# Two PSUM banks for the small steps, two instead of three for the score units, and new places for the steps

## Time and profile before

| what | value |
|---|---|
| median of 3 runs | 1191.55 us (1189.46 to 1191.91) |
| the profiled execution | 1190.55 us |
| its span, first to last instruction | 1188.7 us |
| granted TensorE clock, mean over the span | 0.919 of 2.4 GHz |
| setup, pass -1 | 0 to 99 us |
| pass 0, layer 0 experts, passes 1 to 9 | 99 to 150, 150 to 217, 217 to 805 us |
| layer 1 experts, passes 10 to 15, end | 805 to 938, 938 to 1173, 1173 to 1189 us |

### The profile page before, as it was taken

One profiled execution on the slowest core, in us unless ns is written; L12 is line 12 of the kernel. 1 busy time (PEld: TensorE's weight loads), 2 busy tenths in 40 slices (PEclk: granted clock), 3 DMA queues, 4 the chain that ended last, 5 costly groups with the idle time before them and its releaser, 6 DMA issues.

```text
span 1188.7 us, 23248 instructions
## 1 busy us (share of the span) xinstructions
PE 1017.7 (86%) x7354; PEld 517.9 (44%) x7354; DVE 786.2 (66%) x2427; ACT 653.2 (55%) x1251; POOL 573.5 (48%) x651
## 2 busy tenths in 40 slices
PE   4879889988989898986788788875999989889986
PEld 2522279532333333331333234444889644444433
DVE  5588922578878787878666676683444577678931
ACT  1204722567757666655566565553344567667764
POOL 5184600246547373627858688742000155437663
PEclk8657989999989999988999899987999999999987
DMA  5852557652323041412214224233888545344411
GB/s 144 221 141 66 146 162 207 210 121 46 98 45 97 23 97 28 106 30 57 71 46 121 53 66 106 62 97 128 237 246 256 134 116 134 77 105 111 91 44 46
DMA packets 122540, 130.55 MB, mean 110 GB/s; under 512 B 13952, under 2 KB 105408, under 8 KB 122208
## 3 DMA queue, kind: packets, MB, share of 16 engines
q1 hardware_dynamic: 115856, 116.09, 37.6%
q0 software_dynamic: 6144, 12.60, 4.0%
q10 hardware_dynamic: 432, 0.52, 0.2%
HBM read 83.13 MB, written 52.48 MB: 114 GB/s over the span
## 4 chain that ended last, share of the span: by engine, by line
PE 46%; POOL 25%; DVE 9%; issue 7%; ACT 5%; DMA 5%; SPq 1%; POOLq 0%; ACTq 0%; DVEq 0%
PE ps_banks L610 6%; POOL tokens L995 5%; PE ps_banks L1719 5%; PE ps_banks L569 5%; PE ps_banks L576 4%; POOL sent L1915 3%; PE ps_banks L615 3%; PE ps_banks L693 3%; PE ps_banks L688 3%; DVE a_neg_max L834 3%; PE ps_banks L1460 2%; PE ps_banks L1474 2%; PE ps_banks L1732 2%; PE ps_banks L654 2%; DMA tokens<-made,at 2%
## 5 line engine op out<-in xcount | busy, mean ns | idle before, releaser
L834 DVE TENSOR_REDUCE a_neg_max<-ps_banks 128x1 f32<-128x512 f32 x512 | 325.6, 683 | 94.8 <-PE ps_banks L576 92.6
L737 ACT ACTIVATE a_probs<-ps_banks 128x512 f32<-128x512 f32 x512 | 283.9, 598 | 153.4 <-PE ps_banks L569 150.9
L576 PE MATMUL ps_banks<-k_strip,q_strip 51*128 51x512 bf16 (+3 forms) x1024 | 308.0, 364 | 30.2 <-DVE a_neg_max L834 27.0
L569 PE MATMUL ps_banks<-q_strip,k_strip 53*128 53x512 bf16 (+3 forms) x1024 | 291.1, 353 | 41.3 <-ACT a_probs L739 16.3
L840 DVE CUSTOM_DVE_ANT_0 a_masked<-ps_banks,mask_wide 128x384 bf16<-128x384 f32 (+3 forms) x512 | 221.7, 486 | 61.2 <-PE ps_banks L576 60.6
L739 ACT ACTIVATE a_probs<-ps_banks 128x512 f32<-128x512 f32 x256 | 144.9, 599 | 76.9 <-PE ps_banks L534 74.8
L576 PEld LDWEIGHTS ps_banks<-k_strip,q_strip 51*128 51x128 bf16 x1024 | 77.0, 95 | 185.7 <-ACT a_probs L737 115.3
L957 POOL CAST a_q_parts<-a_q_whole 128x512 bf16<-128x512 f32 x16 | 9.7, 608 | 296.9 <-ACT a_q_whole L770 296.9
L569 PEld LDWEIGHTS ps_banks<-q_strip,k_strip 53*128 53x128 bf16 x1024 | 75.6, 94 | 165.3 <-ACT a_probs L737 52.5
L610 PE MATMUL ps_banks<-a_probs,v_aug 128*32 128x512 f32 x1024 | 141.6, 626 | 0.0
L995 POOL DMA_INDIRECT tokens<-made,at x96 | 93.1, 969 | 27.9 <-issue 27.2
(11 more groups left out here) (248 smaller groups left out, 1680.9 us busy)
## 6 DMA issues: line engine op xcount, KB each, us to landing
work<-in_pack SPq DMA_DIRECT2D x40, 450.0 KB, 3.5
q_rows<-a_q_parts SPq DMA_DIRECT2D x96, 128.0 KB
k_rows<-a_k_parts SPq DMA_DIRECT2D x96, 128.0 KB
q_strip<-q_rows SPq DMA_DIRECT2D x64, 192.0 KB
k_strip<-k_rows SPq DMA_DIRECT2D x64, 192.0 KB
work<-in_w SPq DMA_DIRECT2D x32, 256.0 KB, 3.1
sent<-in_zeros SPq DMA_DIRECT2D x14, 512.0 KB, 7.6
work<-sent SPq DMA_DIRECT2D x56, 128.0 KB, 3.2
```

The lines of the kernel that those rows point to most:

```text
L569: mm = pe.matmul(sbank[:, at:at + hi - lo], k_now[rows(js, ROW_END), slot, kt * P:(kt + 1) * P], q_now[rows(js, ROW_END), slot, lo:hi], st ...
L576: mm = pe.matmul(mbank[:, at:at + hi - lo], q_next[rows(jm, ROW_SHIFT), slot, qt * P:(qt + 1) * P], k_next[rows(jm, ROW_SHIFT), slot, lo:h ...
L737: act.activation(probs[si // 4 % 2][:, si % 4, :], bank, ACT.Exp).then_inc(sems["probs"], 1)
L834: dve.tensor_reduce(neg_max[:, half, qt, hd:hd + 1], bank, AX.X, ALU.max, negate=True).then_inc(sems["max_out"], 1)
```

## The change

- **Banks.** Score units have 2 banks (0, 1), maximum units 3 (2 to 4), the small steps 2 (5, 6) and the sums bank 7. Small steps alternate between banks 5 and 6, each with its own semaphore (`misc_free0`, `misc_free1`); `claim` waits for the last reader of its own bank only. Where a step reads what the step before it had copied out, `after` waits for that copy. Where all must be read out, `all_free` waits for both.
- **Places.** In `MISC[0]`, `shift` is moved ahead of `norm`, `gather` from place 7 to 12 (after `ln1`, which goes from 9 to 10), `yT` from 15 to 16, `ff1` from 16, 17, 19, 20 to 17, 18, 20, 21, `ff2a`/`ff2` from 22, 23 to 23, 24, `ln2` from 25 to 27. In layer 1, `tanh`, `gz`, `mix` and `store` of passes 10 to 13 go from 23, 25, 26, 29 to 27, 28, 29, 31. The parts of the routing are moved by zero to three places.
- **Moments.** They are steps of their own, `pmom` (places 8 and 9) and `fmom` (places 25 and 26), half of the instructions in each; before, they followed the addition at once.
- **Matmuls of `q`, `k` and `ff1`** are issued as two of 256 columns in place of one of 512.
- **The end.** `final` is replaced by `tail_take`, `tail_norm`, `tail_turn`, `tail_out`, each in two halves with banks of its own, and the last `tanh` moves from place 28 to 31, after the last unit.

```diff
-BANKS, RING, MAX_BANK, SUM_BANK, MISC_BANK = 8, 3, 3, 6, 7
+BANKS, LAG, SCORE_RING, MAX_RING, MAX_BANK, MISC_BANK, SUM_BANK = 8, 3, 2, 3, 2, 5, 7
 MISC = {
-    0: {0: [("zTa", 2)], 1: [("ln3a", -2), ("zT", 2)], 2: [("norm", -1, QT - 1)], 3: [("ln3b", -2), ("shift", 0, 1)], 4: [("q", 2)],
-        5: [("onT", -1)], 6: [("k", 2)], 7: [("proj", -1), ("gather", -1)], 8: [("v", 1), ("load", 3)], 9: [("ln1", -1), ("x2T", -2)],
-        10: [("norm", 0, 0)], 11: [("logits", -2)], 12: [("z", 1)], 15: [("yT", -1)], 16: [("fetch", 2, 0), ("ff1", -1, 0)],
-        17: [("ff1", -1, 1)], 18: [("norm", 0, 1)], 19: [("ff1", -1, 2)], 20: [("ff1", -1, 3)], 21: [("shift", 1, 0)],
-        22: [("gate", -1), ("ff2a", -1)], 23: [("ff2", -1)], 24: [("tanh", -1)], 25: [("ln2", -1)], 26: [("norm", 0, 2), ("gz", -1)], 28: [("mix", -1)],
-        30: [("store", -1)]},
-    1: {0: [("zT", 2)], 2: [("shift", 0, 1)], 3: [("q", 2)], 4: [("norm", -1, QT - 1)], 5: [("k", 2)], 7: [("onT", -1)],
-        8: [("v", 1)], 10: [("proj", -1)], 12: [("norm", 0, 0)], 16: [("fetch", 2, 0)], 19: [("shift", 1, 0)], 20: [("norm", 0, 1)],
-        28: [("norm", 0, 2)]},
+    0: {0: [("zTa", 2)], 1: [("ln3a", -2), ("zT", 2)], 2: [("shift", 0, 1)], 3: [("ln3b", -2), ("norm", -1, QT - 1)], 4: [("q", 2)],
+        5: [("onT", -1)], 6: [("k", 2)], 7: [("proj", -1)], 8: [("pmom", -1, 0), ("v", 1), ("load", 3)], 9: [("pmom", -1, 1), ("x2T", -2)],
+        10: [("ln1", -1), ("z", 1)], 11: [("logits", -2)], 12: [("gather", -1), ("norm", 0, 0)], 16: [("yT", -1), ("fetch", 2, 0)],
+        17: [("ff1", -1, 0)], 18: [("ff1", -1, 1)], 19: [("norm", 0, 1)], 20: [("ff1", -1, 2)], 21: [("ff1", -1, 3)],
+        22: [("shift", 1, 0)], 23: [("gate", -1), ("ff2a", -1)], 24: [("ff2", -1)], 25: [("tanh", -1), ("fmom", -1, 0)], 26: [("fmom", -1, 1)],
+        27: [("ln2", -1), ("norm", 0, 2), ("gz", -1)], 29: [("mix", -1)], 31: [("store", -1)]},
+    1: {0: [("zT", 2)], 2: [("shift", 0, 1)], 3: [("norm", -1, QT - 1)], 4: [("q", 2)], 5: [("k", 2)], 7: [("onT", -1)],
+        8: [("v", 1)], 10: [("proj", -1)], 13: [("norm", 0, 0)], 16: [("fetch", 2, 0)], 19: [("shift", 1, 0)], 21: [("norm", 0, 1)],
+        29: [("norm", 0, 2)]},
 }
...
-    NB - 3: routed(0, (13, 14, 16, 19), 27, 29, 30, 28, 31),
-    NB - 2: sends(0, *4 * (0,), *4 * (16,), *4 * (30,)),
-    NB - 1: merged(routed(1, (12, 13, 15, 16), 18, 20, 21, 22, 24), sends(12, *4 * (16,), *4 * (30,))),
-    NB: sends(20, *4 * (17,)),
-    ROUTE1: merged(routed(2, (8, 9, 10, 11), 13, 15, 16, 18, 20), sends(24, *8 * (17,))),
-    **{MIX1 + i: mixed(-2, 8, 20, 23, 25, 26, 29) for i in range(4)},
-    MIX1 + 4: merged(mixed(-2, 0, 8, 11, 13, 14, 17), mixed(-1, 15, 24, 27, 29, 30, 31)),
-    STREAM - 1: merged(mixed(-1, 0, 8, 11, 13, 14, 17), mixed(0, 18, 25, 28, 30)),
+    NB - 3: routed(0, (13, 15, 18, 21), 25, 29, 30, 28, 31),
+    NB - 2: sends(0, *4 * (0,), *4 * (13,), *4 * (30,)),
+    NB - 1: merged(routed(1, (12, 13, 15, 16), 18, 21, 22, 23, 25), sends(12, *4 * (17,), *4 * (30,))),
+    NB: sends(20, *4 * (18,)),
+    ROUTE1: merged(routed(2, (8, 9, 10, 11), 14, 17, 18, 20, 22), sends(24, *8 * (19,))),
+    **{MIX1 + i: mixed(-2, 8, 20, 27, 28, 29, 31) for i in range(4)},
+    MIX1 + 4: merged(mixed(-2, 0, 8, 12, 13, 14, 17), mixed(-1, 15, 24, 30, 31, 31, 31)),
+    STREAM - 1: merged(mixed(-1, 0, 8, 14, 15, 16, 18), mixed(0, 19, 25, 31, 31)),
...
+        def all_free(eng, n):
+            for side in range(2):
+                wait(eng, misc_free[side], n.freed(side))
+        def after(eng, n, made):
+            if made in n.last:
+                side, count = n.last[made]
+                wait(eng, misc_free[side], count)
...
                 def claim():
-                    wait(pe, sems["misc_free"], n.at("misc_free"))
+                    wait(pe, misc_free[n.side()], n.freed(n.side()))
...
-                                wait(pe, sems["probs"], n.at("probs") - (RING - 1))
+                                wait(pe, sems["probs"], n.at("probs") - (SCORE_RING - 1))
...
                         if name in ("q", "k"):
+                            after(pe, n, "zT")
...
-                            pe.matmul(ps_misc, w_of[layer][name][:], z_T[par][:], start=True, stop=True).then_inc(sems["misc"], 1)
+                            for half in (slice(0, S // 2), slice(S // 2, S)):
+                                mm = pe.matmul(ps_misc[:, half], w_of[layer][name][:], z_T[par][:, half], start=True, stop=True)
+                            mm.then_inc(sems["misc"], 1)
...
-                            wait(dve, sems["misc_free"], n.at("misc_free") + 1)
-                            moments_of("ff2", t0, D, QT)
+                        if name == "fmom":
+                            if arg == 0:
+                                all_free(dve, n)
+                            op = moments_of("fmom", t0, D, 2 * arg, 2 * (arg + 1))
+                            if arg == 1:
+                                op.then_inc(sems["moments"], 1)
```

224 lines of the change are left out of this document (147 added, 77 removed).

## The result

The changed kernel takes 1184.37 us (median of 7 runs, 1183.05 to 1187.40); the kernel before took 1191.55 us (median of 7, 1189.46 to 1195.22). The ratio is 0.994, with a 95% interval from 0.9919 to 0.9962. So it is faster, but by 7 us (0.6%) and not by 25.

What follows compares the result with a forecast made beforehand. The prediction took PE to pace the kernel, counting where it stands still. Its terms, +8 - 9 - 9 - 10 - 6 + 1 = -25 us against 1190.55, gave 1165.5 us (1166 for a median), range 1150 to 1185.

Steps and rivals of the forecast that it cites:

- The end: Passes 14, 15 and tail: POOL's last gate stays, sums finish before it, copies and projection run in halves; -6 us.
- Rival 4: Groups without steps: short waits of the two-bank score ring drop PE to the low clock; +42 us, 1208; chance 0.12.
- Passes 10 to 13: Later `tanh` removes most of PE's stall and slow clock: -3.3 us in each of 10 to 12, 0 in 13; -10.
- +1.0 for the score ring: Passes 10 to 12: cost of two score banks in place of three, 1.0 us in each pass.
- Passes 1 to 4: Bank waits, `yT` wait, burst and slow clock go, the score ring costs 2.6 us: -2.2 us each, -9 in all.
- Groups 25, 26 and 27, 28 cost nothing, as DVE is later there: Passes 1 to 4, places 25 to 28: two score banks add no time, since DVE is later; 0 us.
- Pass 0: Few small steps, so two score banks cost 10.1 us, less two waits of `norm` at 1 us each; +8 us.
- Passes 5 to 9: Gathers moved behind `ln1` shorten the chain of PE, DVE and POOL: -8, -3.6, +1.2 and +1.5 us; -9 in all.
- +1.5: From pass 8 to the last `send`: late moments, `ln3a` blocking DVE in pass 9 and later `count`; +1.5 us.
- Rival 2: POOL takes the gains back: passes 5 to 9 give 0, passes 10 to 12 keep their stall; 1182 us; chance 0.15.
- Rival 1: Two score banks are as good as free, as DVE's maxima already hold every group; 1144 us; chance 0.12.
- Rival 3: The second bank for small steps brings nothing, since steps follow one another through their data; 1189 us; chance 0.04.

Runs made afterwards that it cites:

- d_fill: The changed kernel with one unneeded 512-column matmul after each score unit of pass 15, to keep PE busy: 1178.88 us, ratio 0.9925.
- c_wholemom: The changed kernel with both halves of the moments at the first of their two places: 1178.30 us, ratio 0.9926.
- a_oldbanks: The changed kernel with the banks of before, three for score units and one for small steps: 1180.99 us, ratio 0.9923.
- r_ring2: The changed kernel with two score banks but only one bank for small steps, bank 5 left empty: 1203.36 us, ratio 1.0106.
- after_again: The changed kernel once more, unchanged, for a second profile: 1183.06 us, ratio 0.9920.
- p_late9: The kernel with banks by pass, with pass 9's last moments and routing about four places later: 1296.53 us, ratio 1.0008, in the later runs.
- after_third: The changed kernel once more, unchanged, in the later runs: 1327.95 us, ratio 1.0241.
- x_mix: The changed kernel with the banks of before up to pass 4 and from pass 10, the new ones in passes 5 to 9: 1166.36 us, ratio 0.9796.

## Why the prediction was wrong

The direction was right, and the measured time lies inside the range, at its upper end; the size was three and a half times too large by the medians, four times by the profiles. By these, 25 forecast stand against 6.2 measured:

| step | forecast | measured |
|---|---|---|
| setup, pass -1 | 0 | +1.6 |
| pass 0 and the experts of layer 0 | +8 | +5.8 - 5.2 = +0.6 |
| passes 1 to 4 | -9 | -3.9 |
| passes 5 to 9 | -9 | -5.3 |
| experts of layer 1 | 0 | +1.6 |
| passes 10 to 13 | -10 | -4.5 |
| passes 14, 15, end | -6 | +3.7 |
| split | +1 | not to be told from 0 |

- **The end (9.7 us off) is the step that failed most**, in two places. It said of POOL's chain "That doesn't move against pass 14": the last gate came 4.35 us later against pass 14, 2.75 of them also at full clock (d_fill), since POOL's `mix` comes later twice in pass 14, the second time for `gz`. And it said "the sums [...] are over by about 1176", that is, it took pass 15 to be as fast as before. The halves of the tail did give 6 us behind the gate, as d_fill and c_wholemom show; but in the changed kernel PE came 5.5 us after the gate, and the tail gave 0.7. Pass 15 took 42.67 us for 34.77, with 19.3 us at the low level for 10.2 and a ring of two. Neither alone explains that: the low clock is there with three banks too (17.1 us in a_oldbanks, without loss at the end), and the ring alone costs 1.9 us. Pass 14 lost 1.8 us, 1.6 of them with its 3.4 us at the low level (d_fill has none).
- **Rival 4** (PE falls to the low clock, from the short waits of a ring of two) had put the fall into the groups without steps and priced it for all passes. Over the whole span the clock rose from 0.919 to 0.923. The Trainium skill's rule (TensorE: Matmul & The Clock Gate, "A second HAM failure mode: psum-queue depth-cycling") has short idle times between groups of matmuls make the clock swing. The trace does not bear it out as the cause here: pass 0, with the ring's short waits, kept 0.96, and pass 15 had its low clock with three banks and was without it in two runs with two.
- **Passes 10 to 13 (5.5 off).** The stalls before `tanh` went, as forecast: a_oldbanks gains 2.6, 3.1 and 3.0 us in passes 10 to 12. That is 2.9 us a pass where the terms for stall and slow clock (2.54 and 1.2) make 3.7. The other term that was mis-sized is "+1.0 for the score ring": it is 1.8 a pass, also in pass 13, which I had put at 0 and which lost 1.5. The second bank gave 0.8 for my 0.65.
- **Passes 1 to 4 (5.1 off).** The part for places was right in sum (9.2 forecast, 10.0 in a_oldbanks) and wrong in cause, which is luck. "The moments in halves [...] the 1.01 us stall goes": whole moments give the same times. The stall went with the places; the timeline of pass 4 shows how: `ff2a` and `ff2` now stand in one group of 6.14 us, in which DVE and ACT run empty. The step that failed is "Groups 25, 26 and 27, 28 cost nothing, as DVE is later there": with DVE no longer late, the ring of two is what is late next, 1.23 us in group 13, for a copy, `tanh` and an exponential in ACT's queue. "Perhaps half of what the slow clock cost" didn't come either: it was to go with the stall, but a stall of 1.10 us stands in its place, and the low clock is as long as before (13.6 us in passes 1 to 4 in both), where a_oldbanks has none. Of the 6.2 us between these two, passes 1 and 3, at full clock, hold only 1.3. The empty group was nearly right (2.97 us for 3.07). The second bank was worth 1.65 for 2.45: the waits did go, as r_ring2 shows (2.42 us in pass 4), but the step took their sum for the pass's gain, and a third of it did not show.
- **Pass 0 (7.4 off, the other way).** The ring costs 7.4 us (a_oldbanks against the changed kernel) for 10.1 forecast, the places give 1.6 for 2: +5.8 in place of +8. But the larger part of the miss is "The expert blocks stay as they are". In the kernel before, the experts' first transpose waits 3.55 us for a DMA, and 6.8 us of slow clock follow; in the changed kernel it comes 0.83 us after the last score unit, with no slow clock. A deadline behind a stretch hides what the stretch loses.
- **Passes 5 to 9 (3.7 off).** From `yT` of pass 5 to that of pass 6 it is 71.9 us for 79.3, 7.4 less (5.3 for the chain and some of 2.5 forecast); from pass 6 to 7 67.5 (65.2 forecast, 68.8 before). Then it is given back: "+1.5" for `ln3a` and what follows was too little, since pass 9 alone lost 2.9 behind x2 (1.8 in after_again and d_fill). p_late9 shows, with the old banks in most passes and in the later runs, that PE's stall there is not the bound either: with the stall gone, the experts begin that much later. Rival 2 had that; its other half, the stalls of `tanh`, didn't come.
- **Rival 1** (the ring is free) is refuted by r_ring2. **Rival 3** (the second bank brings nothing) too: it is worth 1.65 us a pass in passes 1 to 4 and 10.6 us in passes 5 to 9.

What stays open: why the old banks with the new places lose 16 us in passes 5 to 9, of which the trace shows 12.4 us of PE's waits for `y` (6.0 in the changed kernel) and 8.4 of DVE's for x2 (5.4 there), but not what makes POOL late. What makes the clock fall in one execution of pass 15 and not in another is open too.

## What to carry to other kernels

When a change takes away one wait, price the next one in the same place with everything that the new wait's engine has in its queue there: the ring of two cost most where the old wait had hidden it. A date that is earlier on the clock of the whole run may be later in its own chain: measure it from the start of its stretch. A stretch with a transfer awaited behind it can lose or gain without any effect; look for that before adding it to the sum. A resource that every pass shares needn't be divided in the same way in every pass: giving the rings by pass was worth 16.7 us over the changed kernel on the same chip (1166.4 for 1183.1), twice what the change itself was. In the later runs the variants with rings by pass are again 18 to 31 us under the changed kernel (1296.5 to 1310.1 for 1328.0).

## What the runs showed of the hardware

**The same kernel took 9% longer in later runs, beside indirect DMAs** (before 1295 to 1301 us for 1190; the changed kernel 1328 for 1184). Passes 1 to 4 took what they did in the first runs (255.6 us for 257.4 in the changed kernel), but pass 6 86.9 for 66.4 and pass 12 48.9 for 39.4. The waits of after_third over the whole span, those that the profile puts down to no instruction of the program ("remote"; the first profile of the same kernel has none):

```profile
DVE a_masked L906 <- remote: 66.4, 16, 7.1
ACT a_probs L796 <- remote: 54.0, 11, 9.5
ACT a_probs L794 <- remote: 36.1, 9, 6.4
DVE a_neg_max L900 <- remote: 19.2, 6, 5.0
```

Counted from the trace, ACT and DVE have 46 such waits of over 1.5 us, 200 us in all; those of them that overlap with one of POOL's indirect DMA instructions hold 197 us. The overlap is not the whole condition: passes 1 to 5, with four such instructions each, have no such wait, passes 6 to 8, with 20 each, six or seven. In one wait (p_late9, pass 11) ACT was idle for 3.96 us though PE had written the bank 2 us before its end. What it is that they wait for was not tested. In those runs the order of the kernels is another, too: the changed kernel is 2.4% slower than before, and the variants with banks by pass (x_mix itself, 2% faster than before, was not run again) are between equal and 0.9% slower. There is no profile of the kernel before from those runs, so which stretch turns the order is open.

**The same instructions can meet another clock.** From pass 10 on the changed kernel and c_wholemom run the same program, and pass 15 took 42.67 us in the one (19.3 us at the low level) and 36.13 in the other (none). Single executions of c_wholemom spread over 1173.7 to 1184.5 us.
